# The second layer's first operands begun 35 slots sooner, in every second slot, beside the last blocks of the first attention

## What is computed

```python
x = x + ga * attn0(norm(x) * (1 + ca) + sa)     # one head of 128, softmax over 512 keys
x = x + gb * ffn0(norm(x) * (1 + cb) + sb)      # FP4 quantised: gate, up, silu, down
x = x + ga1 * attn1(norm(x) * (1 + ca1) + sa1)  # 16 heads of 8, causal, with a bias of line incidences
x = x + gb1 * ffn1(norm(x) * (1 + cb1) + sb1)   # ternary weights, 128 -> 512 -> 512 -> 512 -> 128

# in attn1, per batch and head: q, k, v; write and read lines from 4 points each
L = p1[i] * p2[j] - p1[j] * p2[i]               # six coordinates (i, j) per line
line = L / max(norm(L), 1e-12)
logits = q k^T / sqrt(8) + (read_line . J write_line) * decay^(distance) * bias_scale
```

## Time and profile before

| | |
|---|---|
| median of 3 runs | 1063.24 us (1062.8 to 1065.88) |
| the profiled execution | 1059.56 us, of it 1058.3 us from the first to the last instruction |
| busy: PE, DVE, ACT, POOL | 869.2, 750.4, 659.3, 401.9 us |
| mean granted clock of TensorE | 0.936 of full speed |
| prepare | to about 32 us |
| layer0 | to about 343 us |
| second attention | about 343.5 to 865 us |
| second feed-forward part | to the end |

### The profile page before, as it was taken

One profiled execution on the slowest core, in us unless ns is written; L12 is line 12 of the kernel. 1 busy time (PEld: TensorE's weight loads), 2 busy tenths in 40 slices (PEclk: granted clock), 3 DMA queues, 4 the chain that ended last, 5 costly groups with the idle time before them and its releaser, 6 DMA issues.

```text
span 1058.3 us, 25490 instructions
## 1 busy us (share of the span) xinstructions
PE 869.2 (82%) x9999; PEld 526.8 (50%) x9999; DVE 750.4 (71%) x1784; ACT 659.3 (62%) x1154; POOL 401.9 (38%) x664
## 2 busy tenths in 40 slices
PE   3577888877556689898989989899988868898987
PEld 1244455544335356565656656566655543444434
DVE  7366788888755778778687776868878647666653
ACT  4366878874522376756657566566666747776865
POOL 3024444444666547355354635437232210101000
PEclk7599999998967599999999999999999989999999
DMA  5000000000116235342523436154353000000000
GB/s 146 9 13 0 1 1 1 1 1 1 51 52 175 55 86 142 87 129 65 146 71 97 121 76 166 43 133 105 97 149 94 3 2 1 20 2 20 1 22 20
DMA packets 70698, 63.60 MB, mean 60 GB/s; under 512 B 30600, under 2 KB 62824, under 8 KB 70576
## 3 DMA queue, kind: packets, MB, share of 16 engines
q1 hardware_dynamic: 70064, 61.90, 22.1%
q10 hardware_dynamic: 512, 0.02, 0.0%
HBM read 34.02 MB, written 27.36 MB: 58 GB/s over the span
## 4 chain that ended last, share of the span: by engine, by line
PE 44%; DVE 11%; issue 6%; ACT 5%; POOL 2%; DVEq 0%; POOLq 0%; ACTq 0%
PE bank L2008 12%; PE bank L1589 7%; PE bank L1564 3%; PE bank L1537 3%; PE bank L1529 3%; PE bank L1545 3%; PE bank L1526 2%; PE bank L1519 2%; DVE bank L1672 1%; ACT 4g L2066 1%; PE bank L1555 1%; DVE 4f L2102 1%; PE bank L1597 1%; PE bank L1552 1%; DVE roots L1238 1%
## 5 line engine op out<-in xcount | busy, mean ns | idle before, releaser
L1750 ACT ACTIVATE ET<-bank 64x512 f32<-64x512 f32 x128 | 75.5, 590 | 101.4 <-PE bank L1555 100.5
L2089 DVE TENSOR_TENSOR act<-4f,act 128x512 f16<-128x512 f32 x96 | 66.4, 692 | 57.3 <-ACT act L2056 57.1
L1745 ACT ACTIVATE ET<-bank 128x768 f32<-128x768 f32 x128 | 103.2, 806 | 2.4
L1672 DVE TENSOR_TENSOR bank<-bank,W 128x256 f32<-128x256 f32 x128 | 54.7, 427 | 50.9 <-PE bank L1519 50.9
L1677 DVE TENSOR_TENSOR bank<-bank,WT 128x256 f32<-128x256 f32 x128 | 55.2, 431 | 49.9 <-PE bank L1545 49.9
L1682 DVE TENSOR_REDUCE mo<-bank 128x4 f32<-128x512 f32 x128 | 87.8, 686 | 2.7 <-PE bank L1529 2.5
L1589 PE MATMUL bank<-ET,vv 128*32 128x128 f32 (+2 forms) x1792 | 89.1, 323 | 0.8 <-DVE O L1707 0.8
L2056 ACT ACTIVATE act<-4f 128x512 f16<-128x512 f32 x96 | 60.4, 630 | 28.3 <-DVE 4f L2102 26.2
L1690 DVE TENSOR_REDUCE mo<-bank 128x3 f32<-128x384 f32 x128 | 70.0, 547 | 0.0
L1691 DVE TENSOR_REDUCE mo<-bank 128x3 f32<-128x384 f32 x128 | 69.9, 546 | 0.0
L1529 PE MATMUL bank<-maskq,identh 128*64 128x512 bf16 x256 | 62.7, 396 | 0.0
(11 more groups left out here) (377 smaller groups left out, 2539.5 us busy)
## 6 DMA issues: line engine op xcount, KB each, us to landing
ring<-scr_q SPq DMA_DIRECT2D x16, 324.0 KB
QO<-scr_q SPq DMA_DIRECT2D x16, 324.0 KB
ring<-scr_a SPq DMA_DIRECT2D x16, 252.0 KB
KA<-scr_a SPq DMA_DIRECT2D x16, 252.0 KB
ring<-scr_k SPq DMA_DIRECT2D x16, 168.0 KB
KB<-scr_k SPq DMA_DIRECT2D x16, 168.0 KB
scr_a<-dk SPq DMA_DIRECT2D x8, 288.0 KB, 2.6
X<-in_x SPq DMA_DIRECT2D x8, 256.0 KB, 5.1
```

Source lines behind the costliest of these rows:

```text
L1672: dve.tensor_tensor(half(psD, 1), half(psD, 1), over(W[:, h * HB:(h + 1) * HB], NT), ALU.mult).then_inc(s_wq, 1)
L1745: act.activation(ET[n % NE][:, T:SEG * P], psXT[:, 0:NP * P], ACT.Exp).then_inc(s_expo, 1)
L1750: act.activation(to[0:HB, :], psDT[0:HB, :], ACT.Exp)
L2089: dve.tensor_tensor(lo, f32_[f % 3], hi, ALU.subtract).then_inc(s_lo, 1)
```

## The change: what it does

The operands begin at slot BEGIN = 124 instead of 159, one step in every second slot instead of two in three, and there are SLOTS = 37 such steps instead of 27. The ten added ones have n = -1 again, so that they step both batches that have begun: batch 1 gets 21 steps in layer0 instead of 11. GpSimd's step lies in the same slot as TensorE's and one before that of VectorE and ScalarE (before: the same as theirs). The zero fills move from the slots 160 to 167 into 145 to 149 and 152 to 154. The waits of the first steps are replaced by waits for single events of the first attention. Its output projection's weights, its output `oT` and its `Y` lie in `dqn`, `dq` and `vv2` instead of `3xh`, `L` and `sq`; GpSimd sets `vv2` to ones in slot 160.

```diff
-    FREE = 159
+    BEGIN, SLOTS, FREE = 124, ahead.slots + 10, 152
     def operands_slot(f, behind):
-        q, r = divmod(f - FREE - behind, 3)
-        n = 2 * q + r - ahead.slots
-        return n if r < 2 and -ahead.slots <= n < 0 else None
+        q, r = divmod(f - BEGIN - behind, 2)
+        return min(q - ahead.slots, -1) if r == 0 and 0 <= q < SLOTS else None
     def slot_pe(f):
         if n == -ahead.slots:
-            pe.wait_ge(first.s_add, B)
+            pe.wait_ge(first.s_v, B)
     def slot_dve(f):
+        if n in (-ahead.slots, -ahead.slots + H):
+            dve.wait_ge(second.s_add, (n + ahead.slots) // H + 1)
         if n is not None:
-            b, begun = divmod(n + ahead.slots, H)
-            if begun == 0:
-                dve.wait_ge(first.s_add, B)
-                dve.wait_ge(second.s_add, b + 1)
             ahead.dve(n)
     def slot_act(f):
+        if f == FREE - 7:
+            act.wait_ge(first.s_pv, B - 1)
+        if f == FREE:
+            act.wait_ge(first.s_pv, B)
+        for begin, which in ((FREE - 7, (0, 4, 2, 6, 3)), (FREE, (1, 5, 7))):
+            if 0 <= f - begin < len(which):
+                ahead.zero_act(which[f - begin])
-        if n == -ahead.slots:
-            act.wait_ge(first.s_add, B)
-        if FREE < f <= FREE + 8:
-            ahead.zero_act(f - FREE - 1)
+        if n == -ahead.slots + 18:
+            act.wait_ge(first.s_proj, B)
     def slot_pool(f):
-        n = operands_slot(f, 1)
-        if n == -ahead.slots:
+        if f == FREE + 8:
             pool.wait_ge(first.s_add, B)
+            ahead.ones_pool()
+        n = operands_slot(f, 0)
...
-    first_weights = roots, xh[:, 0:D], c.sb("bq", 2, at=held), s_w0
-    first_room = raw_.bitcast(F32)[:, 0:T], raw_.bitcast(F32)[:, T:2 * T], L[:, 0:T], sq[:, 0:T]
+    first_weights = roots, dqn_.bitcast(F32)[:, 0:D], c.sb("bq", 2, at=held), s_w0
+    first_room = raw_.bitcast(F32)[:, 0:T], raw_.bitcast(F32)[:, T:2 * T], dq_.bitcast(F32), vv[2][:, 0:T]
...
+    def ones_pool():
+        pool.memset(vv[2], 1.0)
```

More of the change, by code:

```diff
@@ L564, in attention0 @@
     first = Thread()
-    first.pe, first.dve, first.act, first.pool, first.s_add, first.signals = on_pe, on_dve, on_act, on_pool, s_add, signals
+    first.pe, first.dve, first.act, first.pool, first.signals = on_pe, on_dve, on_act, on_pool, signals
+    first.s_v, first.s_pv, first.s_proj, first.s_add = s_v, s_pv, s_proj, s_add
     return first
@@ L1423, in constants_pool @@
             pool.memset(x, -3e38)
-        for x in vv:
+        for x in vv[0:2]:
             pool.memset(x, 1.0)
+    def ones_pool():
+        pool.memset(vv[2], 1.0)
     def tables_dve():
@@ L1466, in attention1 @@
     ahead.decay_act, ahead.powers_act, ahead.constants_pool = decay_act, powers_act, constants_pool
-    ahead.tables_dve, ahead.complete_dve = tables_dve, complete_dve
+    ahead.tables_dve, ahead.complete_dve, ahead.ones_pool = tables_dve, complete_dve, ones_pool
     ahead.slots = H + AHEAD
```

## The result

The changed kernel takes 1068.07 us (median of 9 runs, 1066.23 to 1069.93), the kernel before on the same chip 1064.4 us (9 runs, 1062.76 to 1066.63): a ratio of 1.0033, 95% interval 1.002 to 1.0045. It is slower by about a third of a per cent, where I forecast 1060.6 us and a range that ended at 1067.5. The profiled execution took 1066.45 us (span 1065.2), that of before 1059.56.

What follows compares the result with a forecast made beforehand. VectorE bounds up to 256 us, behind that something that is no engine's load. Layer0 +4.7 us and second attention -7.3 make -2.6, put on the 1063.24 us median: 1060.6 us; range 1057.5 to 1064, with rivals 1055.5 to 1067.5.

Steps and rivals of the forecast that it cites:

- The second attention: Start of the second attention: without batch 1's roots, transposes and decays it runs 7.3 us sooner, bounds 5 and 9.
- rival 3: Second attention's free slots stay unused, TensorE at 1.2 GHz and a late transfer: gain only 4 us, 1063.9 us, chance 0.12.
- Layer0, up to slot 157 (batch 0's chain): Layer0 to batch 0's decayed product: slot 157 comes at 266.4 us against 256.8 before, 9.6 us late.
- so the chain begins at 240.5: Start of batch 0's chain: points stored about 239.0 us, plus 1.5 us for ScalarE's delayed exponentials.
- 22.7 + 1.3 + 1.9: Length of batch 0's chain in us: products to normalised L, one more operation, then on to VectorE's decayed products.
- the exclusion: VectorE and GpSimd lock each other out for whole instructions beside the attention; bounds 0 and 9 us for batch 0.
- VectorE's share, taken as 3 us: Contention with GpSimd during batch 0's steps beside the attention, 3 us with bounds 0 and 9.
- 57.4 between the two decayed products: Layer0 from slot 157 to 189: 26.9 + 3.9 us to slot 175, then 26.6 for batch 1's chain.
- From batch 1's product to the end of the layer: Layer0 from slot 189 to the barrier: 9.2 us and 14.3 us, ending at 347.3 us.
- ScalarE's first `dk`: Slots 157 to 175: this copy waits for the constant rows until 275.9 us, 2.4 us of stall, net 0.
- Rival 2: Exclusion of VectorE and GpSimd costs 9 us instead of 3 between slots 143 and 168: 1066.6 us, chance 0.18.
- a barrier beyond 352 us: Sign at layer0's end that the sum is wrong on the slow side, by contention; barrier forecast near 347.

Runs made afterwards that it cites:

- hm_and_late_37: Changed kernel, all 37 steps, GpSimd's second product set one slot later behind `hm`, steps from the decayed product on two slots later: 1065.36 us.
- hm_and_late: begin_only with GpSimd's second product set one slot later behind `hm` and all steps from the decayed product on two slots later: 1052.17 us.
- begin_only: Changed kernel with 27 operand steps instead of 37, batch 1 finished in the second attention as before: 1060.0 us, ratio 0.9946 to 0.9977.
- extra_reads: Kernel before with 16 useless GpSimd additions of two operands beside the first attention's last blocks: 1074.11 us, ratio 1.0075 to 1.0123.
- rooms_only: Kernel before with only the first attention's weights, `oT` and `Y` in the changed kernel's rooms, nothing moved: 1064.03 us.

## Why the prediction was wrong

**The second attention (right).** -7.3 forecast, -7.15 measured (6.1 in the first eight blocks, 1.05 in the next); rival 3 is out.

**The step that failed: "Layer0, up to slot 157 (batch 0's chain)".** 266.4 us forecast, 272.35 measured: 5.95 of the 7.6 us by which the layer's end missed the forecast (12.3 against 4.7). Two parts. *Its start*, "so the chain begins at 240.5", was 3.8 us late: 1.2 us as the points were stored only at 241.7 (ScalarE's row at 241.14, 0.60 long), and 2.5 as I had not asked what GpSimd's queue held ahead of the products then (`X + 2Y` to 242.4, an idle for VectorE's `ve`, `rstd` to 244.1). *Its length*, 22.7 + 1.3 + 1.9, was 2.2 us short: the 28 rows of GpSimd's own chain add up to 21.5 us there and to 19.0 before. I had counted the exclusion for VectorE only; GpSimd's operations were longer too, and GpSimd was the chain: its products of 1.24 and 1.25 us, 0.59 elsewhere, ran beside VectorE's L591 and L600, which have two operands in SBUF, as the long ones before had. VectorE's share, taken as 3 us, was about right (3.6). That most of this term carries to the end is in line with hm_and_late_37: 3.8 us less at slot 159 made the layer 2.7 us shorter (145.11 to 142.46).

**The stretches behind it.** 57.4 between the two decayed products against 57.55 is right in sum, by luck: batch 1's products began 29.5 us behind batch 0's decayed one, forecast 31.4, and its chain took 28.1, forecast 26.0. From batch 1's product to the end of the layer 23.5 was forecast and 24.9 came (1.4 us; `hq` and batch 1's remainders share GpSimd at 338.8 to 341.9). ScalarE's first `dk` waited 1.16 us for the constant rows, forecast 2.4; the last zero fill ended at 264.0 where I had placed it at 259.5, and `dk` came at 280.5.

**Rival 2 (its number near, its mechanism only in part).** It named 1066.6 us, by 9 us of exclusion between the slots 143 and 168. Exclusion is 3.6 us up to slot 159 and 7.2 over the whole layer, and hm_and_late shows a kernel with the same exclusion as begin_only that is 8 us faster. It is real (extra_reads), but does not decide here. The prediction's own sign for it, a barrier beyond 352 us, came (354.8) and misled: the barrier was late for several reasons, of which this is one.

**What I took for one thing and was two.** I added the early start (begin_only: -4) to the ten steps (+8) in one chain and saw neither sign. That batch 0 is late is affordable: begin_only has the same slot 159 and wins. The ten steps are not: a tail without the attention has one half batch in flight, and what of batch 1 stands in its queues adds to its chain: 15.4 us (20.3 in the improved order) go for 7.15. Which of batch 1's operations cost how much stays open; 3.2 us of queueing at one `hq` are seen.

**The rest.** The new rooms cost nothing that can be measured (rooms_only, 0.9982 to 1.0015). The spread of the steady part added 1.7 us in this profile (the last block's multiply is 6.8 us late, block 16's 5.1); the medians differ by 3.7.

## What to carry to other kernels

Before moving a chain between engines, write down what stands ahead of each of its operations in every queue and what it then stands ahead of; a two-slot shift of the later steps was worth more (6.8 us, by three runs) than the 35-slot move (4). Split a change into its parts and forecast each sign: here a start 35 slots sooner gained 4 us and its extension lost 8. A wait at an engine proves no cost; take it away, and look whether another wait stands in its place. And when profiles differ, compare TensorE's granted clock over the same rows before the order gets the credit.

## What the runs showed of the hardware

GpSimd's work is not free beside a full VectorE: 19 to 24 us of it in long operations lengthened VectorE's steps by 10 to 13 us, fills included, with reductions (855 ns) and the products that read a bank (512 ns before, 509 with the additions) untouched. GpSimd's operations grow too: the same 128x192 product took 0.59 or 1.25 us. Where TensorE's granted clock was 0.50 instead of 0.96, the same last product of the feed-forward part came 6.5 instead of 4.75 us behind its `hq`.
